# A graph network on one core: the four quarters' wide rows of the second convolution, swept quarter by quarter or summed together per block

## The reference, cut to what matters

```
def _gcn_conv(x, src, dst, norm, W, b, n_nodes):
    h = x @ W
    msg = h[src] * norm[:, None]
    out = jax.ops.segment_sum(msg, dst, num_segments=n_nodes)   # a sum per destination node
    return out + b
# self loops are added to the edges; norm = deg^-1/2[src] * deg^-1/2[dst]
h = relu(_gcn_conv(h, src, dst, norm, W1, b1, n))    # 32 -> 128 features
h = relu(_gcn_conv(h, src, dst, norm, W2, b2, n))    # 128 -> 128
h = relu(_gcn_conv(h, src, dst, norm, W3, b3, n))    # 128 -> 32
```

## Time and profile before

| | |
|---|---|
| median of three runs | 8447.68 us |
| profiled execution | 8391.05 us, span 8389.1 us |
| PE, DVE, POOL, ACT busy | 67%, 56%, 40%, 30% of the span |
| mean granted TensorE clock | 0.805 of 2.4 GHz |
| first gather of P3 / last head | 1960.4 us / 2234.0 us |
| first instruction of POOL in P4 | 2412.23 us |

### The profile page before, as it was taken

One profiled execution on the slowest core, in us unless ns is written; L12 is line 12 of the kernel. 1 busy time (PEld: TensorE's weight loads), 2 busy tenths in 40 slices (PEclk: granted clock), 3 DMA queues, 4 the chain that ended last, 5 costly groups with the idle time before them and its releaser, 6 DMA issues.

```text
span 8389.1 us, 71084 instructions
## 1 busy us (share of the span) xinstructions
PE 5600.4 (67%) x21156; PEld 2560.6 (31%) x21156; DVE 4673.9 (56%) x6891; ACT 2488.2 (30%) x4074; POOL 3325.6 (40%) x3602
## 2 busy tenths in 40 slices
PE   2997885442478555676767676666665799999950
PEld 1433432121133212222222222223454444444410
DVE  5563332232346566686868687783475466666640
ACT  1663332110133211111111111113321366666630
POOL 3777755565425332544434343436207100000026
PEclk9997887655558677887879788887797899999975
DMA  2003557897668677897979787885103000000000
GB/s 78 11 9 131 212 191 105 76 74 63 78 143 167 162 245 248 210 271 197 264 204 268 207 259 224 246 251 46 27 16 13 14 13 14 14 13 16 11 18 19
DMA packets 556098, 1012.47 MB, mean 121 GB/s; under 512 B 100847, under 2 KB 294659, under 8 KB 555332
## 3 DMA queue, kind: packets, MB, share of 16 engines
q1 hardware_dynamic: 449092, 949.90, 31.9%
q0 software_dynamic: 106624, 58.02, 18.6%
HBM read 804.35 MB, written 203.60 MB: 120 GB/s over the span
## 4 chain that ended last, share of the span: by engine, by line
PE 37%; DMA 18%; POOL 14%; issue 13%; DVE 12%; ACT 4%; SPq 1%; POOLq 0%; DVEq 0%; ACTq 0%
POOL gathered L843 8%; DMA gathered<-table,idx_slot 6%; DMA blocks<-net 6%; PE ps L967 5%; PE ps L1355 4%; PE ps L1029 4%; DMA ring<-net 4%; POOL pair_slot L843 2%; PE ps L1117 2%; DVE ring L2152 2%; PE ps L1118 2%; POOL last_of L858 2%; POOL out_dram L951 2%; PE ps L1122 1%; PE ps L1475 1%
## 5 line engine op out<-in xcount | busy, mean ns | idle before, releaser
L843 POOL DMA_INDIRECT gathered<-table,idx_slot x2156 | 2100.7, 974 | 1581.0 <-DVE ring L2152 885.7
L2152 DVE TENSOR_TENSOR ring<-ring,ps 128x1024 f32<-128x1024 f32 (+2 forms) x1008 | 1072.6, 1083 | 464.6 <-DMA ring<-net 428.9
L1029 PE MATMUL ps<-ring,mats 128*32 128x512 f32 (+2 forms) x4032 | 711.9, 654 | 372.7 <-DVE ring L2152 299.8
L967 PE MATMUL ps<-mats,gathered 128*128 128x128 f32 x1029 | 219.6, 357 | 980.9 <-DMA gathered<-table,idx_slot 946.5
L946 POOL COPY idx_slot<-idx_run_end 128x16 int32<-128x16 int32 (+2 forms) x14 | 2.7, 194 | 1556.3 <-SPq L825 1538.5
L967 PE MATMUL ps<-mats,w 128*128 128x128 f32 x1323 | 302.4, 377 | 459.4 <-DVE w L2631 250.2
L967 PEld LDWEIGHTS ps<-mats,gathered 128*128 128x128 f32 x1029 | 146.2, 177 | 1148.1 <-DMA gathered<-table,idx_slot 1056.6
L836 POOL COPY idx_slot<-idx_row 128x16 int32<-128x16 int32 (+2 forms) x154 | 32.4, 211 | 1086.8 <-SPq L554 1041.0
L2219 DVE SCALAR_TENSOR_TENSOR x_block<-ps,bias,blocks 128x512 f32<-128x512 f32 x300 | 224.7, 749 | 381.7 <-PE ps L1122 381.4
L1029 PEld LDWEIGHTS ps<-ring,mats 128*32 128x32 f32 x4032 | 155.9, 125 | 876.1 <-issue 547.0
L2152 DVE TENSOR_TENSOR blocks<-blocks,ps 128x1024 f32<-128x1024 f32 (+2 forms) x336 | 358.4, 1085 | 83.1 <-DMA blocks<-net 79.5
(11 more groups left out here) (277 smaller groups left out, 11928.8 us busy)
## 6 DMA issues: line engine op xcount, KB each, us to landing
ring<-net SPq DMA_DIRECT2D x792, 512.0 KB, 6.4
blocks<-net SPq DMA_DIRECT2D x264, 512.0 KB
net<-ring SPq DMA_DIRECT2D x176, 512.0 KB, 2.8
table<-w SPq DMA_DIRECT2D x165, 256.0 KB, 2.7
gathered<-table,idx_slot POOLq DMA_INDIRECT x2352, 4.6
ring<-net SPq DMA_DIRECT2D x144, 256.0 KB, 3.5
ring<-d_sp SPq DMA_DIRECT2D x122, 256.0 KB, 4.4
x_sp<-x_block SPq DMA_DIRECT2D x79, 256.0 KB, 8.6
```

What stands on the lines that cost most here:

```text
L843: pool.indirect_dma_start(dests(k), None, rows, bass.IndirectOffsetOnAxis(ap=dst[:, k:k + 1], axis=0)).then_inc(done, 16)
L967: last = nc.tensor.transpose(dst[:, k * P:k * P + P], src[:, k * P:k * P + P], mat["ident"])
L1029: last = mm(message[t * D:t * D + D, 0:wd(i)], adders[2 * m + c], ring[slot][:, c * wd(i):(c + 1) * wd(i)], start=(m == 0 and c == 0), sto ...
L2152: v.tensor_tensor(pair, pair, state, ALU.mult).then_inc(sig["pr"][S_], 1)
```

## The change: what it does

All four quarters of block i are now taken before block i + 1, so all wide work stands between the light blocks; the double buffers go by the parity of the quarter instead of the block. The carry cannot run on from one quarter to the next any more, since they advance together: `carry4` has a column per quarter, each starts at 0, and only after the last block is what a quarter's first, unfinished run lacks known. `first_run_rows` finds once the row of that run's end for each quarter (the length of the run is the sum of `first`, which is 1 up to the quarter's first run start; if there is none, a spare last row of `table4`). `join_quarters` takes each quarter's final carry to the next quarter (through a quarter that is one single run, `one_run` passes it on), PE turns it, POOL gathers the rows from `table4`, DVE adds, and POOL scatters them back. SP and POOL start P4 only after that scatter. `products` waits for the scan two quarters back instead of ACT's copy; that wait moved to `wide_rows`, and the scan waits for the transposes two quarters back. SP loads the degree factors two quarters ahead.

```diff
-    n4 = tuple(T * h for h in halves(EB))
-    add("T3", "ld_d4 b1 b1r bk bm b3 b3t b4 st_tab4", blocks=n4)
+    add("T3", "ld_d4 b1 b1r bk bm b3 b3t b4 st_tab4", blocks=(EB * T // 2, EB * T // 2))
...
-    table4 = dram("table4", (1 + EC, T, P))
+    table4 = dram("table4", (2 + EC, T, P))
...
+            sp.dma_start(table4[EC + 1:EC + 2].rearrange("a t f -> a (t f)"), scan[0:1, 0:T * P]).then_inc(s_start, 16)
...
             degrees_in(0)
-            wide_degrees_in(0, 0)
...
-            sweeps = [(t, i) for t in range(1, T) for i in range(EB)]
-            wide_degrees_in(*sweeps[0])
-            wide_rows_out(0, EB - 1)
-            for n, (t, i) in enumerate(sweeps):
-                if n + 1 < len(sweeps):
-                    wide_degrees_in(*sweeps[n + 1])
-                wide_rows_out(t, i)
+            for step in quarter_steps[0:2]:
+                wide_degrees_in(*step)
+            degrees_in(1)
+            for n, (i, t) in enumerate(quarter_steps):
+                if t == 0 and i + 2 < EB:
+                    degrees_in(i + 2)
+                if n + 2 < len(quarter_steps):
+                    wide_degrees_in(*quarter_steps[n + 2])
+                wide_rows_out(i, t)
             for par in (0, 1):
                 stored(sp, "st_tab4", par, q.last("st_tab4", par) + 1)
             sp.sem_inc(s_table, 1)
+            sp.wait_ge(s_sc[0], gathered_by(halves(EB)[0], 0) + 16)
+            settle(sp)
...
             pool.wait_ge(s_table, 4)
+            pool.wait_ge(s_set, SET_DVE + 6)
+            settle(pool)
+            pool.indirect_dma_start(G[0][S_][:, 0:P], None, table4.rearrange("r t f -> (r t) f"),
+                                    bass.IndirectOffsetOnAxis(ap=idx_first_run[:, 0:1], axis=0)).then_inc(s_tg[0], 16)
+            pool.wait_ge(s_set, SET_DVE + 13)
+            settle(pool)
+            pool.indirect_dma_start(table4.rearrange("r t f -> (r t) f"),
+                                    bass.IndirectOffsetOnAxis(ap=idx_first_run[:, 0:1], axis=0), w[0][1][:, 0:P], None
+                                    ).then_inc(s_sc[0], 16)
+            pool.wait_ge(s_sc[0], gathered_by(halves(EB)[0], 0) + 16)
+            settle(pool)
...
-            def products(t, i):
-                par, n = i % 2, q.n("b4", i % 2, i // 2, t * halves(EB)[i % 2])
+            def products(i, t):
+                par, n = t % 2, turn_of(i, t)
                 rows = quarter_rows(t)
-                pe.wait_ge(sig["b4"][par], n + CREDIT)
+                pe.wait_ge(sig["b3"][par], q.n("b3", par, n) + CREDIT)
...
-            def wide_rows(t, i):
+            def wide_rows(i, t):
+                par, n = t % 2, turn_of(i, t)
+                pe.wait_ge(sig["b3"][par], q.n("b3", par, n) + 1 + CREDIT)
+                pe.wait_ge(sig["b4"][par], q.n("b4", par, n) + CREDIT)
                 turn(fit(pD[par], i), w[3][par], q_of(i)).then_inc(sig["b3t"][par], 1)
...
+            light_head(0)
             for i in range(EB):
+                if i + 1 < EB:
+                    light_head(i + 1)
+                products(i, 0)
+                for t in range(T):
+                    if t + 1 < T:
+                        products(i, t + 1)
+                    wide_rows(i, t)
+                if i == 0:
+                    for t in range(T):
+                        last = mm(pB[D_][:, t:t + 1], mat[f"spread{t}"], first_end[:], start=True, stop=True)
+                    last.then_inc(s_pset, 1)
+            pe.wait_ge(s_set, SET_DVE + 12)
+            turn(pB[D_][:, 0:P], w[0][0], 1).then_inc(s_pset, 1)
+            pe.wait_ge(s_set, SET_DVE + 13)
...
+            for i in range(EB):
+                hidden(i, 0)
+                for t in range(T):
+                    if t + 1 < T:
+                        hidden(i, t + 1)
+                    rows_copy(i, t)
...
+            def wide_sums(i, t):
+                par, n = t % 2, turn_of(i, t)
...
+                dve.wait_ge(sig["b3t"][par], q4.n("b3t", par, n) + CREDIT)
+                dve.wait_ge(s_end4, (i - 1) * T + t + 3 if i else 2)
+                v.tensor_tensor_scan(fit(w[3][par], i), fit(pC[par], i), fit(w[2][par], i), carry4[:, t:t + 1], ALU.mult, ALU.add
                                      ).then_inc(sig["b3"][par], 1)
...
+            def first_run_rows():
+                dve.wait_ge(s_pset, SET_PE + 1)
+                v.tensor_copy(one_run[:], pB[D_][:, 0:T]).then_inc(s_set, 1)
+                v.tensor_reduce(run_len[:], first[:], AX_X, ALU.add).then_inc(s_set, 1)
...
+            def join_quarters():
+                dve.wait_ge(s_end4, 2 + T * EB)
+                v.memset(w[0][0][:, 0:D], 0.0).then_inc(s_set, 1)
+                v.tensor_copy(w[0][0][:, D:2 * D], carry4[:, 0:1].to_broadcast([P, D])).then_inc(s_set, 1)
+                v.scalar_tensor_tensor(carry_in[:, 2:3], carry4[:, 0:1], one_run[:, 1:2], carry4[:, 1:2], ALU.mult, ALU.add
+                                       ).then_inc(s_set, 1)
...
+                dve.wait_ge(s_pset, SET_PE + 2)
+                dve.wait_ge(s_tg[0], gathered_by(halves(EB)[0], 0) + 16)
+                v.tensor_tensor(w[0][1][:, 0:P], G[0][S_][:, 0:P], pB[D_][:, 0:P], ALU.add).then_inc(s_set, 1)
...
                 if i:
-                    wide_sums(0, i - 1)
-            wide_sums(0, EB - 1)
-            for t in range(1, T):
-                for i in range(EB):
-                    wide_sums(t, i)
+                    for t in range(T):
+                        wide_sums(i - 1, t)
+                if i == 3:
+                    first_run_rows()
+            for t in range(T):
+                wide_sums(EB - 1, t)
+            join_quarters()
```

More of the change, by code:

```diff
@@ L398, in gnn_kernel @@
         conv_second = [[ring[4 + k][:, u * WB:u * WB + WB] for u in SPACES] for k in (0, 1)]
-        carry4 = first_end
+        carry4, carry_in, one_run = sb("carry4", [P, T]), sb("carry_in", [P, T]), sb("one_run", [P, T])
+        run_len, run_none, quarter_of = sb("run_len", [P, 1]), sb("run_none", [P, 1]), sb("quarter_of", [P, 1])
+        idx_first_run = sb("idx_first_run", [P, 1], I32)
+        SET_DVE, SET_PE = 18, 5
+        quarter_steps = [(i, t) for i in range(EB) for t in range(T)]
+        turn_of = lambda i, t: i * (T // 2) + t // 2
         quarter_rows = lambda t: slice(t * D, t * D + D)
@@ L848, in _ @@
             pool.wait_ge(s_set, 18)
[L849 removed]
+            pool.wait_ge(s_start, 64)
             def body(i, par, j):
@@ L1901, in _, with hidden, rows_copy @@
             q = p_["T3"]
[L1902 to L1916, removed]
+            def hidden(i, t):
+                par = t % 2
+                act.wait_ge(sig["b1"][par], q.n("b1", par, turn_of(i, t)) + 1 + CREDIT)
+                f(fit(w[1][par], i), fit(pA[par], i), ACT.Relu, bias=one_col("b1")).then_inc(sig["b1r"][par], 1)
+            def rows_copy(i, t):
+                par, n = t % 2, turn_of(i, t)
+                act.wait_ge(sig["b3t"][par], q.n("b3t", par, n) + 1 + CREDIT)
+                stored(act, "st_tab4", par, q.n("st_tab4", par, n))
+                f(fit(w[4][par], i), fit(pD[par], i), ACT.Copy).then_inc(sig["b4"][par], 1)
+            for i in range(EB):
[4 more added lines that the diff above has]
+                    rows_copy(i, t)
             q = p_["P4"]
@@ L2469, in _ @@
             q, q4 = p_["P3"], p_["T3"]
[L2471 to L2474, removed]
+            def wide_sums(i, t):
+                par, n = t % 2, turn_of(i, t)
+                dve.wait_ge(sig["b1r"][par], q4.n("b1r", par, n) + 1 + CREDIT)
+                landed(dve, "ld_d4", par, q4.n("ld_d4", par, n))
@@ new lines, in wide_sums @@
+                dve.wait_ge(sig["b3"][par], q4.n("b3", par, n) + 1 + CREDIT)
+                v.tensor_copy(carry4[:, t:t + 1], w[3][par][:, wd(i) - 1:wd(i)]).then_inc(s_end4, 1)
+            def first_run_rows():
[3 more added lines that the diff above has]
+                for t in range(T):
+                    last = v.memset(quarter_of[quarter_rows(t), :], float(t))
+                last.then_inc(s_set, 1)
+                dve.wait_ge(s_set, SET_DVE + 3)
+                v.tensor_scalar(run_none[:], run_len[:], 0.0, float((EC + 1) * T), ALU.is_equal, ALU.mult).then_inc(s_set, 1)
+                v.scalar_tensor_tensor(run_len[:], run_len[:], float(T), quarter_of[:], ALU.mult, ALU.add).then_inc(s_set, 1)
+                dve.wait_ge(s_set, SET_DVE + 5)
+                v.tensor_tensor(idx_first_run[:], run_len[:], run_none[:], ALU.add).then_inc(s_set, 1)
```

49 lines of the change are left out of this document (15 added, 34 removed).

## The result

| | before | after |
|---|---|---|
| median of the runs | 8446.78 us (8431.44 to 8465.1, 4 runs) | 8369.92 us (8360.65 to 8381.82, 4 runs) |
| ratio | | 0.9907, 95% interval 0.9893 to 0.992 |
| profiled execution, span | 8389.1 us | 8380.0 us |
| P3's first POOL copy to P4's | 452.8 us | 383.1 us |

The change brings 77 us, and 132 were forecast. Its own stage is 69.7 us shorter in the two profiles, where 132 to 136 were expected. (The profiled execution of after was an unlucky one outside the stage: P1 and P2 took 658 us in it and everything from P4 on 6014. Against before on their own chips these two runs, one execution each, bring 76 and 108 us.)

A forecast was written before the change was run, and what follows sets the result against it. No engine bounds the whole; P3's stage is paced by gathers, then a 4.15 us loop per block. 135.7 us saved minus 4 for gathers gives 132, 133 at the median's pace: 8447.68 to 8315 us; range 8295 to 8335, 8282 to 8366 for 8 in 10.

The forecast's parts named there:

- The gathers on PE, POOL and DVE beside the wide work: P3's steady blocks: wide work, about 18.5 us a block, fits under the gathers' 22.25 us and costs nothing.
- The tail: After the last gathers: blocks 11 to 13 still due, their last store landed at 2269.4 us.
- The mending: New step before P4: POOL gather, DVE add, POOL scatter and release; 7.1 us, bounds 6.4 and 14.
- The reduction: DVE's sum over 6272 columns after block 3: 6.69 to 13.4 us, hidden at no cost.
- What the gathers pay: P3's gathers beside three times the loads and stores: they give way, costing 4 us, bounds 0 and 42.
- The 0.31 against 0.48 us per packet: Engine time per gather packet in 3400 to 3440 against P3's first half, taken as showing that gathers give way.
- The bound of 42 us: Second rival, 6%: the DMA engines' time in P3 adds up, 290/0.93 - 270 = 42 us, giving 8357 us.
- landings pace the blocks: First rival, 14%: load landings set P3's block pace; 12 us landings give 8345 us, 15 us give +55, 8370.
- its mark of 10.3: First rival: landings beside P3's gathers decide the block pace once they exceed 10.3 us.
- the 3 that I had set: First rival's sign: DVE's multiply waits for its load for over 3 us per quarter.
- second and fourth rivals: In P3: DMA engine time adds up (6%, 8357 us); gathers slowed until nothing is won (7%).
- The other rivals: In P3: gathers slowed until nothing is won (7%: 4% slower, 3% no change); PE's clock rises (7%, 8304 us).

The follow-up runs named there:

- 12: The changed kernel with 512 zero rows used by P3's gathers alone, third chip: 8266.39 us, stage 297.5 us.
- 9: The changed kernel as it is, run on the third chip as measure: 8323.87 us, stage 368.9 us.
- 15: The changed kernel as it is, run on the fourth chip as measure: 8305.08 us, stage 366.7 us.
- 13: The changed kernel with each store of wide rows cut to its first 128 rows, fourth chip: 8335.56 us, stage 332.1 us.
- 10: The changed kernel with P3's degree-factor loads cut from 512 columns to 16, third chip: 8309.59 us, stage 360.4 us.
- 11: The changed kernel with four degree-factor buffers instead of two, loads four steps ahead, third chip: 8311.82 us, stage 362.7 us.
- 14: The changed kernel with stores cut as in 13 and four degree-factor buffers, fourth chip: 8315.27 us, stage 330.7 us.
- 2: The kernel before with 512 zero rows instead of one: 7968.49 us, ratio to before 0.9432; stage 441.7 us.
- 5: The changed kernel with 512 zero rows for P3's gathers alone, second chip (before there 9119.32 us): 9026.9 us, stage 345.2 us.
- 6: The changed kernel with 4 zero rows in one 512-byte line, second chip (before there 9119.32 us): 8859.42 us, stage 348.9 us.
- 7: The changed kernel with 16 zero rows in four adjacent 512-byte lines, second chip (before there 9119.32 us): 8728.78 us, stage 344.0 us.
- 1: The changed kernel with 512 zero rows instead of one: 7826.05 us, ratio to before 0.9264; stage 298.4 us to the mending gather.

## Why the prediction was wrong

- **The gathers on PE, POOL and DVE beside the wide work**: right in kind. Four scans stand between two heads, PE stays at 0.50 of the clock, and with spread rows the heads are 19.9 to 23.1 us apart (12), beside the 22.25 forecast. Where PE works off a backlog, heads are 16.2 to 17.3 us apart; 16.4 to 16.9 were forecast for a block without cover.
- **The tail**: right. From PE's head of block 12 to the last landing 45.6 us were forecast (2223.80 to 2269.4), and 2313.43 to 2359.04 (mending gather) is 45.6. A step is 3.39 us (forecast 3.5), the short block took 10.3 us for 10.0.
- **The mending**: forecast 7.1 us, 2359.04 to 2365.77 is 6.73. The 0.2 us of waking-up before the scatter was an estimate of mine that no row shows: it is 0.81 us from the add's end to the scatter's start, while the gather, from its start to the add, took 2.84 us for the 3.5 forecast.
- **The reduction**: at least 6.69, 6.68 measured, and hidden: ACT stood behind a store until 2089.18, 3.5 us past its end.
- **What the gathers pay**: this is the step that failed: "So the gathers' share gives way." 4 us was taken, and the head of block 12 came 330.7 us after P3's start instead of 264.4: 66 us, and 59 and 57 in 9 and 15. It is the whole miss of the stage, since the terms behind it met to 1 us. The 0.31 against 0.48 us per packet came from the earlier trace rows against the earlier trace rows, and I read it as an effect of the load beside it. In the runs the gathers kept their engine time (200 us, 190 in 9; 184.7 before) and the direct transfers landed later (loads in 9.6 us for 6.0, stores in 9.7 for 6.8); and the one row sets most of a packet's time in both places (0.51 to 0.066 us in P3, 0.25 to 0.035 in the long passes). Why a packet is dearer in P3 than in the long passes isn't shown; that the reads of one row follow each other more closely there (23 packets per us against 18.8) is a likely reason.
- **The bound of 42 us** (the second rival) had the right addends and the wrong divisor. 290 us was the sum; after shows (0.594 + 0.261) x 337 = 288. But the engines were full to 0.855, not to the 0.93 that I had assumed, and 290 / 0.855 is 339 us, 69 more than 270. That this sum meets the number is no proof that engine time is what binds. Over each whole stage, both queues held the engines for 296 us in 15 and 259 in 13, which won 34.5 us: that fits. They held them for 295 us in 9, 279 in 10, which won 8.5, and 307 in 11, which won 6.2 with more engine time: that does not.
- **The rival "landings pace the blocks"** came nearest in its mechanism. In the long gaps landings are 16 to 25 us, over its mark of 10.3, and DVE waits for loads up to 15.3 us; averaged over the stretch neither sign is met (9.6 us, and 135.5 / 49 = 2.8 us a quarter against the 3 that I had set). The sign set for the second and fourth rivals, heads more than 25 us apart, came (28.5). Its 8370 is luck: by its own formula, two loops of landing + 0.8 us in a block, 15 us landings give 31.6 us a block and 84 us over nine blocks, 8399, not +55. It named the load and its two buffers, and four buffers bring 6.2 us (11). What is slow is each direct transfer beside hot gathers, loads and stores (8.8 us both in 9, 4.1 and 2.5 in 12) and SP's issuing, and SP issues them in one order; with deeper load buffers the wait moves to the stores (11, 14). How an engine shares its time between the two queues was not shown. A load's bytes hardly counted in its landing (10: 8.0 us for 8.8, the same 128 packets at 1/32 of the bytes). But the number of packets is no price by itself: in 9 a store of 512 packets and a load of 128 both land in 8.8 us.
- **The other rivals**: a gather packet's engine time grew from 0.476 us to 0.51, 1.07 times, far from the 1.26 at which the change would be within 0.5% of nothing; the clock did not rise (0.50 throughout the stage).
- **Where rows differ** the change brings 142 us, 10 more than the forecast.

Shown: the one zero row costs the changed kernel 71 us in P3's stage (12 against 9), of which before pays 11 as well (2), and both kernels about 480 to 540 us in all. Still open: by which way it stretches the stage. Smaller stores bring 35 us; smaller loads 8.5 and deeper load buffers 6.2 were tried only one by one with full stores; the rest was not pulled apart. Why the waits pile up at three blocks and not at the others was not looked into, nor was a second issuing engine for the stores tried.

The fastest version that was run is the changed kernel with 512 zero rows: 7826.05 us.

## What to carry to other kernels

Before queueing direct transfers beside gathers, divide the gather queue's engine time by its packets: 0.5 us a packet was here not traffic but many indices that named one row, and 512 copies of that row cost four instructions and two small DMAs in the setup. DMA engines idle to 20% in the stretch's mean before were not free here for small transfers (256 KB loads landed in 3.6 us without the gathers, in 6.0 beside them and in 9.6 with the change's own there as well): look at landings with and without the neighbour, look for the longest landings and not the median alone, and price new transfers at the crowded value, in the order in which one queue issues them. And when one stall is seen to have two possible origins in a trace (here 0.31 against 0.48 us), look at the data behind the addresses before trusting the friendlier one.

## What the runs showed of the hardware

- A packet of the gather queue held its engine for less time the more zero rows stood in for the one. In the long passes (4800 to 5000): 0.25 us with one row (after; 0.24 in 5), 0.12 with four neighbouring rows (6), 0.054 with sixteen (7), 0.035 with 512 (1). In P3's stage: 0.51 us with one row (after) and 0.066 with 512 (1). These are means over packets of 1024 and of 4 bytes, half of each.
- The hot gathers did not give way to direct traffic: 184.7 us of engine time before (1960 to 2230), 200 in after (1983 to 2320) beside three times as many direct packets. With loads of 1/32 of the bytes they took 211 us for 190 (10, 9), with smaller stores 186 for 191 (13, 15), so no rule comes out of it.
- Beside the hot row direct packets held their engines no longer than beside spread ones (89 us for all of them in 9, 103 in 12), and still a 256 KB load landed in 8.8 us (9) instead of 4.1 (12).
- SP's issue of one load took up to 5.1 us in after's stage (6.2 in 9, and 7.1 for a store), where the median in before, 2245 to 2405, is 0.37 us; with spread rows (12) it stayed under 1 us within the gathers' part.
- TensorE at 80% busy for 165 us and at 49% for 347 us (after) stayed at 0.50 of the clock, as in the profile of every other run of this stage.
- Four chips gave 8400, 8413, 8447 and 9119 us for the kernel before (the first two are one execution each).
